# An adaLN attention and sparse-FFN kernel: full shapes for the last group's expert marks, and a new order of work on four engines

## The chip, the cores and the metric

The kernel runs on one core of a Trainium2 chip. The metric is the device time of one execution in microseconds (us): 114.97 us before the change, the median of three executions (114.91 to 114.98).

## The reference, cut to what matters

One transformer block over 2048 tokens of width 128. The values stay in full f32 precision, which the kernel reaches by splitting each operand into a rounded high part and a low rest.

```python
h = layernorm(x) * (1 + ca) + sa
q, k, v = (h @ Wq + bq) / sqrt(128), h @ Wk + bk, h @ Wv + bv
x = x + ga * (softmax(causal(q @ k.T)) @ v @ Wo + bo)
h = layernorm(x) * (1 + cb) + sb
prob = softmax(h @ w_router + b_router)         # 16 expert blocks of 32 channels
mask = top 4 blocks of each token
y = relu(h @ w1.T + b1)                         # 512 channels
x = x + gb * ((y * mask of its block) @ w2.T + b2)
```

## The kernel before, in words

The tokens are worked in four groups of 512 (`GW`), each of four tiles of 128. The order of work is written out by hand: for each engine a plan (`TENSOR_PLAN`, `SCALAR_PLAN`, `VECTOR_PLAN`, `GPSIMD_PLAN`) lists words, a letter for a step and a number for which one. Each engine runs its words strictly in that order, and semaphores hold an instruction until its inputs are there. So a word that waits holds all words behind it on its engine.

The words that matter here, on TensorE: `z` prepares weights, `n` turns a normalized group so that channels are on partitions (4 transposes), `q` projects queries, `a` scores 128 rows to find the row maxima, `b` turns those maxima, `p` and `s` make the score tiles that are used, `w` multiplies the exponentials of a tile by the values, `o` is the output projection, `r` the router's logits, `m` turns the choice of experts, `h` computes 128 hidden channels of a group (4 per group, h12 to h15 for the last), `v` closes the channels of unchosen experts, `d` multiplies by w2, `y` turns the result back, `t` computes the last two tiles in another way. Nearly all matmuls are three passes over 512 columns (L928, L929, L932: high by high, low by high, high by low).

On ScalarE `e` are the exponentials, `a` the normalizations, `c` the copy of the attention sums, `m` the copy of the turned choice, `h` the high part of a hidden chunk, `y` the copy of a result. On GpSimd (POOL) `z` makes constants, `j` and `p` compute the inverse square roots for the norms, `u` splits the tokens, `l` makes the low part of an exponential tile (L512), `k` the low part of a hidden chunk (L518). On VectorE `g` are the norm's statistics, `s` the row maxima, `i` the causal mask on a tile, `x` the output of attention, `m` and `c` the choice of four experts, `h` the masked hidden chunk, `k` and `f` low parts and final sums.

The first three groups multiply the hidden values by a mask (`keep`, [128 channels x 512 tokens]) on VectorE. The last group does it on TensorE: `choose` marks the experts a token did not choose (`unchosen`, 16 columns a tile), `turn_choice` transposes these marks (word m3, L1103, 4 transposes of 16 columns), ScalarE copies them to `shut` (16 partitions x 512), and `shut_channels` (words v12 to v15, L1133) adds a matmul of `spread` (16 x 128, with -1e30 at each expert's channels) by `shut` to the hidden chunk before the relu. This matmul contracts over 16 rows only, in bf16, between matmuls that contract over 128 rows in f32. `spread` is made at the start by GpSimd's word z4 (L502 to L507).

Of the kernel before, what the change touches and what calls it, by code (L numbers as in the profile page):

```python
# [42 lines left out]
TENSOR_PLAN = """
i1 i0 i3 z0 i2 z10 z1 n0 z2 z6 z3 q0 z4 z7 a0 a1 a2 a3 n1 p2 p1 p0 b0 q1 s0 s1 a4 a5 z5 s2 a6 s3 a7 n2 w0 a8 a9
w1 w2 w3 a10 a11 p4 z9 p6 z8 b1 q2 o0 n3 s4 a12 p5 a13 s5 s6 a14 s7 a15 a16 w4 s8 a17 w5 a18 s9 a19 q3 a20 s10
a21 w6 a22 s11 a23 w7 a24 w8 b2 w9 a25 w10 s12 a26 s13 a27 s14 w11 s15 a28 a29 w12 s16 o1 s17 s18 s19 a30 a31
s20 w13 s21 a32 w14 a33 s22 a34 w15 a35 s23 w16 a36 a37 w17 w18 a38 a39 n4 w19 w20 b3 w21 r0 w22 s24 s25 h0 z11
s26 w23 s27 s28 m0 s29 w24 n5 o2 s30 s31 h1 s32 r1 w25 w26 w27 h2 s33 w28 s34 w29 m1 w30 h3 n6 s35 s36 s37 r2
s38 w31 w32 w33 h4 w34 w35 w36 s39 m2 w37 w38 w39 h5 d0 o3 d1 d2 d3 h6 h7 d4 h8 d5 h9 d6 n7 d7 h10 r3 d8 h11 d9
d10 m3 y0 h12 v12 h13 v13 y1 d11 h14 v14 h15 v15 d12 d13 y2 d14 d15 t0 y3 t1  # L50
"""
# [6 lines left out]
VECTOR_PLAN = """
j0 z0 j1 a0 z1 a1 g1 z3 u0 u1 z10 g2 v1 s0 s1 s2 s3 q0 n1 b0 g3 s4 s5 z5 s6 s7 q1 s8 s9 s10 s11 n2 b1 x0 s12 s13
s14 q2 s15 s16 n3 s17 i8 s18 s19 i9 s20 s21 i10 s22 s23 s24 i11 b2 s25 z6 s26 s27 q3 s28 s29 g4 x1 g5 s30 i20  # L60
s31 s32 s33 s34 s35 i21 s36 s37 i22 s38 s39 n4 i23 b3 m0 c0 h0 x2 n5 g6 h1 m1 c1 n6 i36 h2 h3 i37 m2 i38 c2 i39
h4 h5 x3 g7 h6 h7 h8 h9 n7 h10 m3 c3 h11 f0 k12 k13 f1 k14 k15 f2 f3 t0 t1
"""
GPSIMD_PLAN = """
z0 z1 z4 j0 j1 u0 p1 z7 p2 z6 z8 l0 l1 l2 p3 u1 z11 u2 l4 l5 l6 l7 l8 l9 z10 l10 l12 l13 l14 l15 l16 l17 l18 p4
l19 l20 l21 p5 l22 z9 u3 l24 l25 l26 l27 l28 l29 l30 p6 l31 k0 l32 l33 k1 l34 l35 l36 k2 l37 l38 k3 k4 k5 p7 k6
k7 k8 k9 k10 k11 z12
"""
# [1206 lines left out]
```

## Time and profile before

| | before |
|---|---|
| time, median of 3 executions | 114.97 us |
| span of the profiled execution | 113.2 us |
| busy: TensorE | 109.0 us (96%) |
| busy: GpSimd | 88.1 us (78%) |
| busy: VectorE | 87.3 us (77%) |
| busy: ScalarE | 74.3 us (66%) |
| chain that ended last | TensorE 81%, VectorE 13%, issue 2%, GpSimd 2% |

The span runs from the first to the last instruction of the program in the profiled execution. The measured time holds 1.8 us more than it (114.97 less 113.2), which is the launch and end around the program; a time of its own is not given for the profiled execution, so its span stands for it. The busy time of TensorE contains waits that the profile cannot separate, since the ends of matmuls are modelled. What an instruction there really took is read from start to start.

### The profile page before, as it was taken

What the parts mean: (1) busy time and instruction counts of PE and PEld (TensorE: products, weight loads), DVE (VectorE), ACT (ScalarE), POOL (GpSimd) and SP (SyncE); (2) the same over time, 40 slices, a digit from 0 to 9 for tenths busy, and PEclk for the clock granted to TensorE, in tenths of its full rate; (3) what the DMA queues carried; (4) which work ended last, traced back from release to release, by engine and by line L of the source; (5) the groups of instructions that cost most, each with busy time, mean ns of one, the idle gap of its engine ahead of it and who ended that gap; (6) DMA issues with size and microseconds to landing.
All of it is one profiled execution on the core that took longest, in us unless ns stands there. A gap on an engine that the chain in (4) does not pass through costs nothing.

```text
span 113.2 us, 2012 instructions
## 1 busy us (share of the span) xinstructions
PE 109.0 (96%) x585; PEld 87.6 (77%) x585; DVE 87.3 (77%) x322; ACT 74.3 (66%) x163; POOL 88.1 (78%) x118
## 2 busy tenths in 40 slices
PE   5999999999999999999999999999999999999991
PEld 2588769878888888888877878788898888856590
DVE  5999989999999999978897399708974846854251
ACT  1346398497973499677498995988815578435610
POOL 6869868998999199989899999999992898916000
PEclk9999999999999999999999999999999999999999
DMA  2894000000000000000000000000000000003314
GB/s 60 266 336 130 3 0 6 0 3 0 0 3 0 6 0 0 0 0 3 0 0 6 0 0 0 0 0 0 0 6 3 0 3 0 0 0 93 98 56 129
DMA packets 5879, 3.42 MB, mean 30 GB/s; under 512 B 743, under 2 KB 5483, under 8 KB 5868
## 3 DMA queue, kind: packets, MB, share of 16 engines
q1 hardware_dynamic: 5292, 3.03, 9.0%
q10 hardware_dynamic: 576, 0.26, 0.9%
q8 instruction: 5, 0.08, 0.3%
q14 instruction: 6, 0.05, 0.1%
HBM read 2.24 MB, written 1.05 MB: 29 GB/s over the span
## 4 chain that ended last, share of the span: by engine, by line
PE 81%; DVE 13%; issue 2%; POOL 2%
PE bank L928 14%; PE bank L929 13%; PE bank L932 13%; PE bank L1040 7%; PE bank L988 7%; PE bank L1027 6%; PE bank L1028 6%; PE bank L1072 3%; PE bank L962 2%; PE bank L1168 2%; PE bank L1139 2%; DVE nmax L743 1%; DVE st L686 1%; POOL rstd L440 1%; PE bank L1133 1%
## 5 line engine op out<-in xcount | busy, mean ns | idle before, releaser
L512 POOL TENSOR_TENSOR p_lo<-p_full,p_hi 128x512 fp32r<-128x512 f32 (+2 forms) x36 | 42.5, 1206 | 4.6 <-ACT p_full L626 4.5
L619 ACT ACTIVATE p_hi<-bank 128x512 fp32r<-128x512 f32 (+2 forms) x36 | 20.6, 571 | 6.6 <-PE bank L932 2.9
L626 ACT ACTIVATE p_full<-bank 128x512 f32<-128x512 f32 (+2 forms) x36 | 20.5, 568 | 0.6 <-POOL p_lo L512 0.6
L518 POOL TENSOR_TENSOR hid_lo<-hid_full,hid_hi 128x512 fp32r<-128x512 f32 x12 | 15.4, 1294 | 5.3 <-ACT hid_hi L655 5.3
L748 DVE TENSOR_REDUCE cmax<-bank 128x1 f32<-128x512 f32 x24 | 16.1, 685 | 2.0 <-PE bank L988 1.7
L1027 PE MATMUL bank<-g_hi,zt_hi 128*128 128x512 f32 (+3 forms) x40 | 15.2, 381 | 0.0
L1040 PE MATMUL bank<-g_lo,zt_hi 128*128 128x512 f32 (+3 forms) x40 | 14.6, 373 | 0.2 <-DVE g_lo L768 0.2
L1028 PE MATMUL bank<-g_hi,zt_lo 128*128 128x512 f32 (+3 forms) x40 | 14.6, 364 | 0.0
L928 PE MATMUL bank<-p_hi,z_hi 128*128 128x512 f32 (+2 forms) x36 | 14.0, 389 | 0.0
L988 PE MATMUL bank<-zt_hi,g_hi 128*128 128x512 f32 (+3 forms) x40 | 13.8, 386 | 0.0
L929 PE MATMUL bank<-p_hi,z_lo 128*128 128x512 f32 (+2 forms) x36 | 13.5, 374 | 0.0
L932 PE MATMUL bank<-p_lo,z_hi 128*128 128x512 f32 (+2 forms) x36 | 13.4, 373 | 0.0
L841 DVE SCALAR_TENSOR_TENSOR hid_full<-bank,keep 128x512 f32<-128x512 f32 x12 | 8.1, 686 | 5.6 <-POOL hid_lo L518 2.7
L590 ACT ACTIVATE xn<-x,mean_rstd,rstd 128x127 f32<-128x127 f32 x24 | 9.9, 485 | 0.3 <-POOL mean_rstd L433 0.3
L655 ACT CAST hid_hi<-hid_full 128x512 fp32r<-128x512 f32 x12 | 7.4, 622 | 3.0 <-DVE hid_full L841 2.4
L1040 PEld LDWEIGHTS bank<-g_lo,zt_hi 128*128 128x128 f32 x40 | 7.5, 188 | 1.8 <-issue 0.7
L988 PEld LDWEIGHTS bank<-zt_hi,g_hi 128*128 128x128 f32 x40 | 7.5, 189 | 1.4 <-ACT g_hi L605 0.2
L1027 PEld LDWEIGHTS bank<-g_hi,zt_hi 128*128 128x128 f32 x40 | 7.5, 189 | 1.1
L1028 PEld LDWEIGHTS bank<-g_hi,zt_lo 128*128 128x128 f32 x40 | 7.6, 189 | 0.9
L430 POOL TENSOR_TENSOR rstd<-rstd,pow_half 128x4 f32<-128x4 f32 x7 | 7.3, 1038 | 0.6
L928 PEld LDWEIGHTS bank<-p_hi,z_hi 128*128 128x128 f32 x36 | 6.8, 188 | 1.2
L932 PEld LDWEIGHTS bank<-p_lo,z_hi 128*128 128x128 f32 x36 | 6.8, 188 | 1.2
(212 smaller groups left out, 256.1 us busy)
## 6 DMA issues: line engine op xcount, KB each, us to landing
x<-in_L_attn_y_all_dram SPq DMA_DIRECT2D x3, 256.0 KB, 3.5
out_dram<-res SPq DMA_DIRECT2D x3, 256.0 KB, 2.3
w<-in_L_ffn_w_dram SPq DMA_DIRECT2D x2, 256.0 KB, 4.2
x<-in_L_attn_y_all_dram SPq DMA_DIRECT2D x2, 128.0 KB, 2.9
wmod<-in_L_wmod_dram SPq DMA_DIRECT2D x1, 256.0 KB, 3.7
wmod<-in_L_wmod_dram ACTq DMA_DIRECT2D x1, 128.0 KB, 3.2
out_dram<-res SPq DMA_DIRECT2D x1, 128.0 KB, 1.9
wk<-in_L_attn_Wk_dram SPq DMA_DIRECT2D x1, 64.0 KB, 2.9
```

Of the source, the lines that this page charges most:

```text
L512: pool.tensor_tensor(p_lo[:, s, w:], p_full[:, n % 2, w:], p_hi[:, s, w:].bitcast(F32), ALU.subtract).then_inc(p_lo_pool, 1)
L518: pool.tensor_tensor(hid_lo[:, m, :], hid_full[:, n % 2, :], hid_hi[:, m, :].bitcast(F32), ALU.subtract).then_inc(hid_lo_pool, 1)
L619: nc.scalar.activation(p_hi[:, s, w:], src, ACT.Exp).then_inc(p_hi_s, 1)
L626: nc.scalar.activation(p_full[:, n % 2, w:], src, ACT.Exp).then_inc(p_full_s, 1)
L748: nc.vector.tensor_reduce(cmax[:, n, c:c + 1], src, AX.X, ALU.max, negate=True).then_inc(turn_out, 1)
L928: mm(dst, w_hi, m_hi, start=start, stop=False)
L929: mm(dst, w_lo, m_hi, start=False, stop=False)
L932: return mm(dst, w_hi, m_lo, start=False, stop=stop)
L988: last = mm(dst[:, 0:w], tile(g_hi, g * GT + r), zt_hi[:, c * GW:c * GW + w], start=True, stop=not masked)
L1027: mm(dst[:, w:], tile(zt_hi, j), high, start=True, stop=False)
L1028: mm(dst[:, w:], tile(zt_lo, j), high, start=False, stop=False)
L1040: last = mm(dst[:, w:], tile(zt_hi, j), g_lo[:, g * GW + w:(g + 1) * GW], start=False, stop=not diag)
```

## The change

The marks and the pattern of the last group are widened with zeros and with the pattern's own continuation to the whole array: `unchosen` has 128 columns a tile, of which 112 are zeroed once at the start by GpSimd, `spread` and `shut` have 128 partitions. The rows beyond the 16th of `shut` are zero, so the sum is the same. The wait for `spread` moves from v12 to m3. All four plans hold the same words as before, in another order.

```diff
-        shut, spread = sb("shut", [NBLK, GW], BF16), sb("spread", [NBLK, P], BF16)
-        spread_full = sb("spread_full", [NBLK, P])
-        unchosen = sb("unchosen", [P, GT, NBLK], BF16)
+        shut, spread = sb("shut", [P, GW], BF16), sb("spread", [P, P], BF16)
+        spread_full = sb("spread_full", [P, P])
+        unchosen = sb("unchosen", [P, GT, P], BF16)
...
                 elif i == 4:
+                    ahead(pool.memset(unchosen[:, :, NBLK:], 0.0))
                     step(pool.memset(spread_full[:], FAR))
...
-                    nc.scalar.copy(shut[:], norm_bank[0:NBLK, 0:GW // 2].bitcast(BF16)).then_inc(keep_s, 1)
+                    nc.scalar.copy(shut[:], norm_bank[:, 0:GW // 2].bitcast(BF16)).then_inc(keep_s, 1)
...
-                    nc.vector.tensor_scalar(unchosen[:], marked[:, :, 0:NBLK], FURTHEST, None, ALU.is_lt).then_inc(chosen_s, 1)
+                    nc.vector.tensor_scalar(unchosen[:, :, 0:NBLK], marked[:, :, 0:NBLK], FURTHEST, None, ALU.is_lt).then_inc(chosen_s, 1)
...
                 if g in shut_by_tensor:
+                    pe.wait_ge(spread_made, 1)
                     for i in range(GT):
-                        last = nc.tensor.transpose(norm_bank[0:NBLK, i * P // 2:(i + 1) * P // 2].bitcast(BF16),
+                        last = nc.tensor.transpose(norm_bank[:, i * P // 2:(i + 1) * P // 2].bitcast(BF16),
                                                    unchosen[:, i], ident_b[:])
...
                 pe.wait_ge(keep_s, n // NH + 1)
-                if n == NH * shut_by_tensor[0]:
-                    pe.wait_ge(spread_made, 1)
                 mm(turned_bank(f"h{n}")[:], spread[:], shut[:], start=False, stop=True).then_inc(turn_mm, 1)
...
 GPSIMD_PLAN = """
-z0 z1 z4 j0 j1 u0 p1 z7 p2 z6 z8 l0 l1 l2 p3 u1 z11 u2 l4 l5 l6 l7 l8 l9 z10 l10 l12 l13 l14 l15 l16 l17 l18 p4
-l19 l20 l21 p5 l22 z9 u3 l24 l25 l26 l27 l28 l29 l30 p6 l31 k0 l32 l33 k1 l34 l35 l36 k2 l37 l38 k3 k4 k5 p7 k6
+z0 z7 z4 j0 j1 z1 p1 u0 p2 z6 l0 l1 l2 p3 u1 u2 z8 l4 l5 l6 l7 z10 l8 l9 l10 z11 l12 l13 l14 l15 l16 p4 l17
+l18 p5 l19 l20 l21 l22 u3 l24 z9 l25 l26 l27 l28 p6 l29 l30 l31 l32 k0 l33 k1 l34 l35 l36 l37 l38 k2 k3 k4 k5
```

Line numbers shift by one behind the inserted line of word z4 (L502), by two behind the wait inserted in `turn_choice`, and by none again behind the two lines taken out of `shut_channels`, so L928, L929, L932 of before are L929, L930, L933 of the changed kernel, and L1103 is L1105; L1133 and L1168 keep theirs.

TensorE near the end, before: m3 (L1103), y0 (L1168), h12, v12 (L1133), h13, v13, y1.

```order
L1103 MATMUL bank<-ident_b,unchosen 16x128 x4
L1168 MATMUL bank<-ident,y_sb 128x128 x4
L928 MATMUL bank<-h_hi,w1t_hi 128x512
L929 MATMUL bank<-h_hi,w1t_lo 128x512
L932 MATMUL bank<-h_lo,w1t_hi 128x512
L1133 MATMUL bank<-shut,spread 128x512
L928 MATMUL bank<-h_hi,w1t_hi 128x512
L929 MATMUL bank<-h_hi,w1t_lo 128x512
L932 MATMUL bank<-h_lo,w1t_hi 128x512
L1133 MATMUL bank<-shut,spread 128x512
L1168 MATMUL bank<-ident,y_sb 128x128 x4
```

The same place in the changed kernel, from the last pass of d9: y0, m3 (L1105), h13, y1, v12 and v13.

```order
L933 MATMUL bank<-hid_lo,w2t_hi 128x512
L1168 MATMUL bank<-ident,y_sb 128x128 x4
L1105 MATMUL bank<-ident_b,unchosen 128x128 x4
L929 MATMUL bank<-h_hi,w1t_hi 128x512
L930 MATMUL bank<-h_hi,w1t_lo 128x512
L933 MATMUL bank<-h_lo,w1t_hi 128x512
L1168 MATMUL bank<-ident,y_sb 128x128 x4
L1133 MATMUL bank<-shut,spread 128x512 x2
```

h12 now stands ahead of d9, the transposes y0 ahead of m3, d10 behind v13, and v12 and v13 follow each other; v14 and v15 still stand alone.

GpSimd at the start of the program, before: z1 (`causal`), z4 (`spread`), and the first inverse square root (j0).

```order
L470 MEMSET causal_full 128x128
L471 AFFINE_SELECT causal_full<-causal_full 128x128
L473 CAST causal<-causal_full 128x128
L502 MEMSET spread_full 16x128
L503 AFFINE_SELECT spread_full<-spread_full 16x128
L505 AFFINE_SELECT spread_full<-spread_full 16x128
L507 CAST spread<-spread_full 16x128
L439 TENSOR_SCALAR rstd<-mv 128x2
```

In the changed kernel: z7 (`future`), the widened z4, j0.

```order
L475 MEMSET future 128x128
L476 AFFINE_SELECT future<-future 128x128
L502 MEMSET unchosen 128x4x112
L503 MEMSET spread_full 128x128
L504 AFFINE_SELECT spread_full<-spread_full 128x128
L506 AFFINE_SELECT spread_full<-spread_full 128x128
L508 CAST spread<-spread_full 128x128
L439 TENSOR_SCALAR rstd<-mv 128x2
```

Ahead of j0 three instructions of `causal` gave way to two of `future` and a memset of 4x112 elements.

GpSimd in the middle, before: l10 to l18 with p4 behind l18 (`p_lo` is a low part of exponentials, L428 to L433 the inverse square root of a second norm).

```order
L512 TENSOR_TENSOR p_lo<-p_full,p_hi 128x512 x7
L428 TENSOR_SCALAR neg_mean<-mv 128x4
L429 TENSOR_SCALAR rstd<-mv 128x4
L430 TENSOR_TENSOR rstd<-rstd,pow_half 128x4
L433 TENSOR_TENSOR mean_rstd<-neg_mean,rstd 128x4
L512 TENSOR_TENSOR p_lo<-p_full,p_hi 128x512 x2
L512 TENSOR_TENSOR p_lo<-p_full,p_hi 128x384
```

In the changed kernel: l12 to l16, p4, l17, l18, p5.

```order
L513 TENSOR_TENSOR p_lo<-p_full,p_hi 128x512 x5
L428 TENSOR_SCALAR neg_mean<-mv 128x4
L429 TENSOR_SCALAR rstd<-mv 128x4
L430 TENSOR_TENSOR rstd<-rstd,pow_half 128x4
L433 TENSOR_TENSOR mean_rstd<-neg_mean,rstd 128x4
L513 TENSOR_TENSOR p_lo<-p_full,p_hi 128x512 x2
L428 TENSOR_SCALAR neg_mean<-mv 128x4
```

Both inverse square roots now stand ahead of l19, which had only p4 ahead of it.

## Rows read from the trace of the kernel before

**Rows 1.** The page, busy time of each engine (us, share of span, instructions).

```profile
PE 109.0 (96%) x585; PEld 87.6 (77%) x585; DVE 87.3 (77%) x322; ACT 74.3 (66%) x163; POOL 88.1 (78%) x118
```

**Rows 2.** The waits of TensorE: who waited for whom, total us, times, longest.

```profile
PE bank L1182 <- DVE lift L876: 0.2, 1, 0.2
PE bank L1040 <- DVE g_lo L768: 0.2, 1, 0.2
```

**Rows 3.** TensorE's timeline at v12 and v15: start us, us, instruction.

```profile
101.29 0.39 PE L932 MATMUL bank<-h_lo,w1t_hi 128*128 128x512 f32 x1
101.61 0.38 PE L1133 MATMUL bank<-shut,spread 16*128 16x512 bf16 x1
101.92 0.50 PE L928 MATMUL bank<-h_hi,w1t_hi 128*128 128x512 f32 x1
102.25 0.39 PE L929 MATMUL bank<-h_hi,w1t_lo 128*128 128x512 f32 x1
...
106.00 0.40 PE L932 MATMUL bank<-h_lo,w1t_hi 128*128 128x512 f32 x1
106.33 0.39 PE L1133 MATMUL bank<-shut,spread 16*128 16x512 bf16 x1
106.64 0.39 PE L928 MATMUL bank<-hid_hi,w2t_hi 128*128 128x256 f32 x1
106.88 0.28 PE L929 MATMUL bank<-hid_hi,w2t_lo 128*128 128x256 f32 x1
```

**Rows 4.** TensorE's timeline at m1, full-shape bf16 transposes of an earlier group.

```profile
73.47 0.39 PE L932 MATMUL bank<-p_lo,z_hi 128*128 128x512 f32 x1
73.70 0.40 PE L1108 MATMUL bank<-ident_b,chosen 128*128 128x128 bf16 x4
73.91 0.48 PE L928 MATMUL bank<-p_hi,z_hi 128*128 128x512 f32 x1
74.23 0.39 PE L929 MATMUL bank<-p_hi,z_lo 128*128 128x512 f32 x1
```

**Rows 5.** Timeline of the weight loads at m1 and at v12.

```profile
73.70 0.23 PEld L1108 LDWEIGHTS bank<-ident_b,chosen 128*128 128x128 bf16 x4 [0.26 <-issue]
...
101.60 0.09 PEld L1133 LDWEIGHTS bank<-shut,spread 16*128 16x128 bf16 x1 [0.36 <-issue]
```

**Rows 6.** TensorE's timeline ahead of m3 and behind y0, and around y2.

```profile
99.68 0.40 PE L932 MATMUL bank<-hid_lo,w2t_hi 128*128 128x512 f32 x1
...
101.06 0.39 PE L929 MATMUL bank<-h_hi,w1t_lo 128*128 128x512 f32 x1
...
107.47 0.60 PE L1168 MATMUL bank<-ident,y_sb 128*128 128x128 f32 x4
...
108.03 0.28 PE L929 MATMUL bank<-hid_hi,w2t_lo 128*128 128x256 f32 x1
```

**Rows 7.** GpSimd's timeline at the start.

```profile
0.36 0.10 POOL L1262 MEMSET const-bfloat16-1.0<- 128x1 bf16 x1
...
1.51 0.21 POOL L470 MEMSET causal_full<- 128x128 f32 x1
...
2.46 0.20 POOL L502 MEMSET spread_full<- 16x128 f32 x1
2.73 0.99 POOL L503 TENSOR_SCALAR_AFFINE_SELECT spread_full<-spread_full 16x128 f32<-16x128 f32 x1
...
4.14 0.28 POOL L507 CAST spread<-spread_full 16x128 bf16<-16x128 f32 x1
4.67 0.25 POOL L439 TENSOR_SCALAR rstd<-mv 128x2 f32<-128x2 f32 x1 [0.25 <-DVE mv L698]
```

**Rows 8.** Timelines in the middle: GpSimd's p4 and l19 to l21, TensorE's last pass of w20.

```profile
48.76 0.24 POOL L428 TENSOR_SCALAR neg_mean<-mv 128x4 f32<-128x4 f32 x1
...
50.65 3.58 POOL L512 TENSOR_TENSOR p_lo<-p_full,p_hi 128x512 fp32r<-128x512 f32 x3
...
55.64 0.40 PE L932 MATMUL bank<-p_lo,z_hi 128*128 128x512 f32 x1
```

More of the change, by code:

```diff
@@ L43 @@
 TENSOR_PLAN = """
[L44 to L48, printed above, removed]
@@ L49 @@
-s38 w31 w32 w33 h4 w34 w35 w36 s39 m2 w37 w38 w39 h5 d0 o3 d1 d2 d3 h6 h7 d4 h8 d5 h9 d6 n7 d7 h10 r3 d8 h11 d9
-d10 m3 y0 h12 v12 h13 v13 y1 d11 h14 v14 h15 v15 d12 d13 y2 d14 d15 t0 y3 t1
+i1 i0 i3 z0 i2 z10 z1 n0 z2 z3 q0 z4 z6 a0 a1 a2 p0 a3 n1 z7 b0 p1 q1 p2 s0 s1 a4 a5 z5 s2 a6 s3 a7 w0 a8 n2
+a9 w1 w2 w3 a10 a11 p4 z9 p6 z8 b1 q2 o0 n3 s4 a12 p5 a13 s5 s6 a14 s7 a15 a16 s8 w4 a17 s9 a18 w5 a19 q3 a20
+s10 a21 w6 a22 s11 a23 w7 a24 w8 b2 w9 w10 s12 a25 s13 w11 a26 s14 a27 s15 o1 s16 s17 a28 w12 a29 s18 a30 s19
@@ L51 @@
+s20 a31 a32 w13 w14 a33 s21 a34 w15 a35 n4 a36 w16 a37 s22 w17 a38 s23 a39 w18 w19 w20 b3 r0 w21 s24 w22 w23
+s25 s26 s27 o2 s28 m0 s29 w24 h0 h1 n5 w25 z11 w26 s30 s31 s32 r1 h2 w27 s33 w28 s34 s35 w29 m1 s36 h3 w30 n6
+s37 w31 s38 w32 h4 s39 r2 w33 w34 w35 w36 w37 w38 w39 h5 d0 m2 o3 d1 d2 d3 h6 h7 d4 d5 h8 h9 d6 n7 h10 d7 r3
+d8 h11 h12 d9 y0 m3 h13 y1 v12 v13 d10 d11 h14 v14 h15 v15 d12 d13 d14 y2 d15 t0 y3 t1
 """
 SCALAR_PLAN = """
-z0 z1 j0 j1 z3 z6 z11 q0 z4 n1 z9 a2 q1 e0 z5 e1 e2 n2 e3 c0 z13 z12 a3 z8 q2 e4 n3 e5 e6 e7 e8 q3 e9 e10 e11
@@ L54 @@
-e12 e13 c1 e14 e15 e16 z7 e17 e18 e19 e20 a4 e21 n4 e22 e23 a5 e24 e25 e26 c2 m0 e27 e28 e29 n5 e30 h0 e31 e32
-a6 h1 e33 m1 e34 n6 e35 e36 e37 z14 h2 h3 e38 e39 c3 h4 m2 h5 y0 h6 h7 a7 h8 n7 h9 y1 h10 m3 h11 h12 h13 y2 h14
-h15 y3 z15
+z0 z1 j0 j1 z3 q0 z11 z4 z6 n1 a2 q1 e0 z9 z5 e1 e2 e3 z13 c0 n2 z12 a3 q2 z8 e4 e5 e6 n3 e7 e8 e9 q3 e10 e11
+e12 c1 e13 e14 e15 e16 e17 e18 a4 e19 z7 e20 n4 e21 e22 e23 e24 c2 e25 e26 a5 e27 m0 e28 n5 h0 e29 e30 e31 h1
+e32 e33 e34 a6 m1 h2 e35 n6 e36 e37 e38 z14 h3 e39 c3 m2 h4 h5 y0 h6 h7 a7 h8 n7 y1 h9 h10 h11 m3 h12 h13 y2
@@ L57 @@
+h14 h15 y3 z15
 """
 VECTOR_PLAN = """
[L59 to L62, printed above, removed]
+j0 z0 j1 a0 z1 a1 g1 u0 z3 u1 z10 g2 v1 s0 s1 s2 s3 q0 n1 b0 g3 s4 s5 z5 s6 s7 q1 s8 s9 s10 s11 n2 b1 x0 s12
@@ L63 @@
+s13 s14 q2 s15 s16 n3 s17 i8 s18 s19 i9 s20 s21 i10 s22 s23 s24 b2 i11 s25 s26 s27 g4 x1 s28 z6 s29 s30 g5 s31
+s32 s33 s34 i20 s35 i21 s36 s37 n4 s38 s39 i22 q3 b3 i23 m0 c0 x2 h0 g6 h1 n5 m1 c1 i36 h2 i37 i38 n6 h3 m2
+i39 c2 h4 h5 x3 g7 h6 h7 h8 h9 n7 h10 m3 c3 h11 f0 f1 k12 k13 k14 k15 f2 t0 f3 t1
 """
 GPSIMD_PLAN = """
-z0 z1 z4 j0 j1 u0 p1 z7 p2 z6 z8 l0 l1 l2 p3 u1 z11 u2 l4 l5 l6 l7 l8 l9 z10 l10 l12 l13 l14 l15 l16 l17 l18 p4
-l19 l20 l21 p5 l22 z9 u3 l24 l25 l26 l27 l28 l29 l30 p6 l31 k0 l32 l33 k1 l34 l35 l36 k2 l37 l38 k3 k4 k5 p7 k6
@@ L67 @@
-k7 k8 k9 k10 k11 z12
+z0 z7 z4 j0 j1 z1 p1 u0 p2 z6 l0 l1 l2 p3 u1 u2 z8 l4 l5 l6 l7 z10 l8 l9 l10 z11 l12 l13 l14 l15 l16 p4 l17
+l18 p5 l19 l20 l21 l22 u3 l24 z9 l25 l26 l27 l28 p6 l29 l30 l31 l32 k0 l33 k1 l34 l35 l36 l37 l38 k2 k3 k4 k5
+p7 k6 k7 k8 k9 k10 k11 z12
 """
```

## Prediction

> **What bounds the kernel now.** I read the page's busy times first. TensorE is busy for 109.0 of 113.2 us, and no other engine passes 78% [rows 1]. Such a busy time can hide waits, so the waits of TensorE come next: there are only two behind the opening, of 0.2 us each, for the first `lift` (L1182) and for the first shift in `g_lo` (L1040), both in the first 16 us [rows 2]. So behind the head TensorE issues one matmul after the other, and the end moves with the sum of its steps. A moved word gains nothing there by itself; it can only lose, where it comes before its input. The third view is TensorE's timeline, read from start to start: three passes of 512 columns follow each other at 0.23 us (73.47 to 73.70, [rows 4]). What takes longer than its columns is lost time that the busy figure hides, and the few bf16 matmuls over 16 rows are such places [rows 3]. VectorE and GpSimd matter in two ways: in the head, where TensorE waits for them, and in the middle, where GpSimd makes the low parts that TensorE reads.
>
> **The full shapes, on TensorE.** The change neither adds nor removes a matmul. In the place of v12 (L1133 by 16 rows) the passes around it start at 101.29, 101.61, 101.92 and 102.25 [rows 3]. From the L932 to the L929 behind it that is 0.96 us. The two f32 passes in it are worth 2 x 0.23 = 0.46, so the visit costs 0.50. Around v15 it is 106.00 to 106.88, 0.88 us; less 0.23 and less 0.12 (256 columns are half of 512) it is 0.53. There are four such visits; at the mean of the first and the last, 0.515, they take 2.06 us.
>
> What they take in full shape is shown by no L1133, but by a bf16 group of the same 512 columns between the same f32 passes: m1, four transposes of 128 columns with all rows and columns. From 73.47 to 74.23 it is 0.76 us; less 0.46 the visit costs 0.30 [rows 4]. The weight loads say why the two differ. At m1 the load starts at 73.70, just as the pass ahead has had its 0.23; at v12 it starts at 101.60, 0.08 behind the 0.23 of the pass ahead (101.29 + 0.23 = 101.52) [rows 3, 5]. Behind v12 the next pass starts 0.31 after it instead of 0.23, and the one after that again 0.33 later. So a partial shape is paid for on entry and on leaving, 0.08 each, and its successor's weights are loaded late as well; a full shape in bf16 pays for its own load alone.
>
> In the changed order v12 and v13 follow each other, so the pair enters once: 0.30 + 0.23 = 0.53. v14 and v15 stand alone, 0.30 each. The sum is 1.13, and the four visits save 2.06 - 1.13 = 0.93 us.
>
> m3 has its 16 columns on the other side, in its output. From the L932 at 99.68 to the L929 at 101.06 it is 1.38 us [rows 6]. In it are two passes, 0.46, and the four transposes of y0, which I price at y2's: 107.47 to 108.03 is 0.56, less the 0.12 of one pass of 256 columns, 0.44. So m3 costs 1.38 - 0.46 - 0.44 = 0.48. As m1 it costs 0.30, a saving of 0.18.
>
> Together 1.11 us. These are all in the last 14 us, where each step stands on the path to the end. Bounds: if the bf16 load hides as well, a v costs its 0.23 alone, four cost 0.92, and m3 costs 0.23: a saving of 1.39. If shape has no part in it, only the pairing helps, 0.515 - 0.23 = 0.29. I take 1.1, since m1 has the types, the columns and the neighbours of the case.
>
> The late load at 101.60 [rows 5] stands against a rule of the Trainium skill, "TensorE: Matmul & The Clock Gate", Step-by-step: what each phase is for: the time of a weight load goes by its number of columns, and its number of rows does not matter. By that rule the widening of `spread` from 16 to 128 rows gains nothing, and the time would be that of the first rival below; by the rows it is that of the sum.
>
> **What the others do for it.** ScalarE's copy `shut` and VectorE's `unchosen` keep their free sizes (512 and 64 elements a partition), so I cost them at nothing. The wait for `spread` ahead of m3 is for something made a hundred microseconds before. v12 waits for ScalarE's copy, which now stands behind the cast h11; in between TensorE has h13 (0.69) and y1 (0.44), and I expect this cover to hold.
>
> **GpSimd's start.** Ahead of the first inverse square root (L439, 4.67) GpSimd idles 0.25 us, from the end of `spread` at 4.42 [rows 7]. Three instructions of `causal` took 1.51 to 2.46, 0.95 us; two of `future` I take at two thirds of that, 0.63. Then comes a memset of 448 elements. One of 1 element takes 0.10, one of 128 elements 0.20, so 448 take 0.10 + 448/128 x 0.10 = 0.45. That makes 1.08 for 0.95, 0.13 later, within the 0.25: nothing. Lower bound 0.20 (a memset does not get slower by length), also nothing. Upper bound: it takes as long as the slowest elementwise instruction of GpSimd in any row here, one split of 512 (3.58 for 2.75 of them, 1.30) [rows 8]: then L439 is 0.63 + 1.30 - 0.95 - 0.25 = 0.73 late, and since the first normalization, the turn and the scores hang on it, so is the end. The affine select of 0.99 us (2.73) is a riddle, as its twin behind it takes 0.3; if it is a collision it can swallow the delay or double it. I take 0.
>
> **The orders.** In the head w1's preparation (z6, z7) moves behind the first query projection and the first maxima. The wait for `g_lo` (0.2) is set by VectorE, whose words there stay but for one swap, so I take 0; at best both waits of [rows 2] go, -0.4. In the middle the tightest place that I find is GpSimd's. Before, p4 alone stands ahead of l19; now p4 and p5 do. p4 takes 48.76 to 50.65, 1.89 us. l19 to l21 then run 50.65 to 54.23, l20 ends at about 50.65 + 2 x 1.30 = 53.25 [rows 8]. With another 1.89 ahead it ends at 55.14. TensorE's w20 reads it in its last pass at 55.64 [rows 8], and the words ahead of w20 on TensorE are the same as before. So 0.5 us of cover is left: cost 0, bound +0.5 if the estimate of GpSimd's queue is 1 us short. ScalarE's a4 now stands ahead of e19 and needs p4; it makes e19 later, and l19 can't start before e19, but l19 is already behind p5.
>
> **The sum.** 113.2 - 1.1 = 112.1 us of span. The measured median stands 1.8 above the span before (1.77), and nothing around the program changes: 113.9 us.
>
> **The rivals.**
> - *Type, not shape.* The lost time at v12 comes from going between f32 and bf16, in whatever shape. Then only the pairing of v12 and v13 gains, 0.29: 114.7 us. Against it stands m1, the same change of type at 0.30 instead of 0.50. For it: no full bf16 matmul of 512 columns stands between f32 passes in this trace. 5%.
> - *The memset is on the head's path.* GpSimd reaches L439 up to 0.73 late: 113.9 + 0.3 to 0.7, 114.2 to 114.6. For it: only 0.25 of idle time, and a select of 0.99 that nothing explains. 13%.
> - *The new orders wait in several places.* The full saving comes, but TensorE, which had no waits behind the head, gets some of 0.1 to 0.2 each where words come earlier than before: half of the gain is lost, 114.2 to 114.7. 9%.
> - *GpSimd's queue becomes the bound in the middle (the slower side).* Both p4 and p5 ahead of l19, and l19 held by e19, which ScalarE reaches only when a4 has had p4's result. The cover at w20 is 0.5. Up to there it costs nothing, beyond it each microsecond costs one; the change turns slower when GpSimd is 0.5 + 1.1 = 1.6 us later than I count. Were p5 to start only after a further p-length (1.89), it would be 1.4 lost against 1.1 gained: 115.3 us. Against it: p5's input comes from VectorE early, by the place that its word has there. 5%.
>
> **How the numbers follow.** The forecast has 68%, with its own range of 113.5 to 114.2: the saving of 1.39 instead of 1.1 and the waits of the head make the low end, some 0.3 of small waits the high one. With the rivals at 5, 13, 9 and 5% the range for 8 in 10 is 113.4 to 114.5, which leaves out the top of the second and third rival and most of the first and the fourth. About 0.2% (0.23 us) is what a measurement of this kernel tells from no change. Faster than that: the forecast 68, the second rival 13, the third 8, half of the first 2: 90 or so, which I round down to 0.88, for what I have not seen in four rewritten orders. The same 0.06, slower 0.06.
>
> **What would show it.** Right: the L1133 are of form 128x512, the step from the pass ahead into them is 0.23, from the load of L1133 to the next f32 load there is almost no time, and from the passes around one v it is 0.76 instead of 0.96; the stretch from d9 to the first of t0 shrinks by about 1.1; TensorE's list of waits has nothing new above 0.2; L439 starts at 4.7. Wrong: L1133 still 0.31 long with a late load behind it (first rival); the start of L439 and all of VectorE's head shifted alike (second); new waits of TensorE for GpSimd's `p_lo` between 50 and 60 us (fourth), or for ScalarE's `shut` ahead of v12.

## The result and the profile after

The change makes the kernel slower: 115.75 us (median of four executions, 115.72 to 115.82) against 114.97 (now four executions, 114.91 to 115.23), a ratio of 1.0065 with a 95% interval of 1.0048 to 1.0081. Forecast was 113.9, so 1.85 us are missing. The profiled execution has a span of 114.0 us and took 115.72.

The busy times, against [rows 1], say little. TensorE is busy for 0.5 us less, where run 1, with the shapes alone, is 1.2 us less busy. VectorE has 2.0 us more, with the same 322 instructions of the same sizes, and that is the first hint:

```profile
PE 108.5 (95%) x585; PEld 87.3 (77%) x585; DVE 89.3 (78%) x322; ACT 74.5 (65%) x163; POOL 89.1 (78%) x119
```

**Where the time went.** Three places of TensorE's program have the same work ahead of them in both orders (but for one or two words): the third pass of s0, m0's transposes and t0. Timeline of TensorE, kernel before and then kernel after:

```profile
15.53 0.47 PE L1040 MATMUL bank<-g_lo,zt_hi 128*128 128x512 f32 x1 [0.19 <-DVE g_lo L768]
...
61.95 0.40 PE L1108 MATMUL bank<-ident_b,chosen 128*128 128x128 bf16 x4
...
108.61 0.39 PE L1139 MATMUL bank<-w_full,hid_last 128*128 128x128 f32 x2
```

```profile
16.45 0.47 PE L1041 MATMUL bank<-g_lo,zt_hi 128*128 128x512 f32 x1
...
63.66 0.40 PE L1110 MATMUL bank<-ident_b,chosen 128*128 128x128 bf16 x4
...
109.45 0.49 PE L1139 MATMUL bank<-w_full,hid_last 128*128 128x128 f32 x3
```

The delay is 0.92 at s0, 1.71 at m0 and 0.84 at t0. At r3, where the last stretch begins, it is still 1.74 (96.22 and 97.96). So the head loses 0.9, the middle another 0.8 (0.2 of the head comes back behind s0, so the middle's own loss is 1.0), and the end gains 0.9, where the shapes alone gain 1.3 (run 1) and a new stall costs 0.3 (runs 9 and 10).

**The end.** TensorE's timeline at v12 and v13, then at v14:

```profile
103.48 0.60 PE L1168 MATMUL bank<-ident,y_sb 128*128 128x128 f32 x4
103.92 0.59 PE L1133 MATMUL bank<-shut,spread 128*128 128x512 bf16 x2
...
104.58 0.39 PE L930 MATMUL bank<-hid_hi,w2t_lo 128*128 128x512 f32 x1
...
106.20 0.40 PE L933 MATMUL bank<-h_lo,w1t_hi 128*128 128x512 f32 x1
106.44 0.39 PE L1133 MATMUL bank<-shut,spread 128*128 128x512 bf16 x1
...
106.91 0.39 PE L930 MATMUL bank<-h_hi,w1t_lo 128*128 128x512 f32 x1
```

From L933 at 106.20 to L930 at 106.91 it is 0.71 with one L1133 in it, where [rows 3] have 0.96. Less two passes of 0.23, a visit costs 0.25 instead of the 0.50 there. What is read is the step over the visit and the pass behind it, since L929's modelled start (106.48) moves with the shape.

**The waits name little of the loss.** TensorE's list of waits, against [rows 2]:

```profile
PE bank L1182 <- DVE lift L877: 0.5, 1, 0.5
PE bank L963 <- DVE xn L714: 0.3, 1, 0.3
...
PE bank L929 <- DVE hid_full L842: 0.2, 1, 0.2
```

What explains it are durations. Three instructions of VectorE (one of v1's, the sum z6, the marks) and one of GpSimd took 1.4 to 5.4 times as long as the same instruction in the kernel before, each beside an instruction of the other of these two engines. Durations of v1 (four instructions), of the marks and of the sum of two rows (ns, lowest, median, highest), kernel before and then kernel after; the last line is GpSimd's low parts:

```profile
L713 DVE TENSOR_SCALAR xn<-x,mv,rstd x4: 316/338/352, 10.9 to 11.7; 128x127 f32<-128x127 f32 x4
L826 DVE TENSOR_SCALAR unchosen<-marked x1: 194/194/194, 99.3 to 99.3; 128x64 bf16<-128x64 f32 x1
L889 DVE TENSOR_TENSOR w_full<-w_full,b_row x1: 1059/1059/1059, 38.7 to 38.7; 1x512 f32<-1x512 f32 x1
L512 POOL TENSOR_TENSOR p_lo<-p_full,p_hi x36: 729/1294/1332, 17.3 to 83.4; 128x512 fp32r<-128x512 f32 x28, 128x384 fp32r<-128x384 f32 x4, 128x256 fp32r<-128x256 f32 x4
```

```profile
L714 DVE TENSOR_SCALAR xn<-x,mv,rstd x4: 333/342/993, 11.2 to 12.6; 128x127 f32<-128x127 f32 x4
L827 DVE TENSOR_SCALAR unchosen<-marked x1: 1044/1044/1044, 101.0 to 101.0; 128x64 bf16<-128x64 f32 x1
L890 DVE TENSOR_TENSOR w_full<-w_full,b_row x1: 1515/1515/1515, 45.4 to 45.4; 1x512 f32<-1x512 f32 x1
L513 POOL TENSOR_TENSOR p_lo<-p_full,p_hi x36: 736/1295/2149, 18.2 to 83.9; 128x512 fp32r<-128x512 f32 x28, 128x384 fp32r<-128x384 f32 x4, 128x256 fp32r<-128x256 f32 x4
```

What GpSimd did meanwhile, from its timeline of the kernel after, beside v1 and beside the marks (what it did beside z6 stands with run 7):

```profile
10.78 1.28 POOL L445 TENSOR_TENSOR z_lo<-xn,z_hi 128x512 fp32r<-128x512 f32 x1
...
99.43 2.54 POOL L519 TENSOR_TENSOR hid_lo<-hid_full,hid_hi 128x512 fp32r<-128x512 f32 x2 [1.22 <-ACT hid_hi L656]
```

The marks start at 100.98 and take 1.04, to 102.02; GpSimd's pair ends at 99.43 + 2.54 = 101.97. So they seem not to have run slowly but to have stood still until GpSimd was done. In the kernel before, the same split u0 ran from 8.19, 1.27 long, and had ended before v1 began at 10.90.

My theory after these traces: the new orders put one-source and two-source VectorE instructions that work in SBUF beside GpSimd's splits, and one stands still for the other. The rivals: the orders place words of TensorE ahead of their inputs; or the wider shapes cost something elsewhere.

### The profile page after: what moved, and what is told of

Its sections match the earlier page's. It is cut to its first block, busy times and chain, and to the rows that moved or that the text cites. A ratio compares the mean times of both kernels' runs of the same rounds, so it can differ in the third digit from the quotient of the medians.

```text
span 114.0 us, 2013 instructions
## 1 busy us (share of the span) xinstructions
PE 108.5 (95%) x585; PEld 87.3 (77%) x585; DVE 89.3 (78%) x322; ACT 74.5 (65%) x163; POOL 89.1 (78%) x119
## 4 chain that ended last, share of the span: by engine, by line
PE 67%; DVE 12%; POOL 6%; DMA 4%; issue 4%; SPq 3%; ACT 1%; DVEq 0%
PE bank L929 10%; PE bank L933 10%; PE bank L930 10%; PE bank L1041 7%; PE bank L989 6%; PE bank L1028 6%; PE bank L1029 6%; POOL hid_lo L519 4%; DMA x<-in_L_attn_y_all_dram 4%; SPq L370 3%; PE bank L1073 2%; PE bank L963 2%; DVE hid_full L842 2%; PE bank L1139 2%; DVE xn L714 1%
## 5 line engine op out<-in xcount | busy, mean ns | idle before, releaser
L513 POOL TENSOR_TENSOR p_lo<-p_full,p_hi 128x512 fp32r<-128x512 f32 (+2 forms) x36 | 43.2, 1227 | 5.1 <-ACT p_full L627 4.8
L989 PE MATMUL bank<-zt_hi,g_hi 128*128 128x512 f32 (+3 forms) x40 | 14.8, 387 | 0.1
L929 PE MATMUL bank<-p_hi,z_hi 128*128 128x512 f32 (+2 forms) x36 | 13.8, 382 | 0.0
L933 PE MATMUL bank<-p_lo,z_hi 128*128 128x512 f32 (+2 forms) x36 | 13.6, 377 | 0.0
L930 PE MATMUL bank<-p_hi,z_lo 128*128 128x512 f32 (+2 forms) x36 | 13.5, 374 | 0.0
L933 PEld LDWEIGHTS bank<-p_lo,z_hi 128*128 128x128 f32 x36 | 6.8, 188 | 1.5 <-POOL p_lo L513 0.3
L930 PEld LDWEIGHTS bank<-p_hi,z_lo 128*128 128x128 f32 x36 | 6.8, 188 | 1.0
```

What stands on the lines that cost most here:

```text
L513: pool.tensor_tensor(p_lo[:, s, w:], p_full[:, n % 2, w:], p_hi[:, s, w:].bitcast(F32), ALU.subtract).then_inc(p_lo_pool, 1)
L929: mm(dst, w_hi, m_hi, start=start, stop=False)
L930: mm(dst, w_lo, m_hi, start=False, stop=False)
L933: return mm(dst, w_hi, m_lo, start=False, stop=stop)
L989: last = mm(dst[:, 0:w], tile(g_hi, g * GT + r), zt_hi[:, c * GW:c * GW + w], start=True, stop=not masked)
```

## The experiments

Twelve kernels ran. "Difference" is against the runs of the kernel before in the same comparison.

| run | edit | median us (runs) | before | difference | ratio, 95% interval |
|---|---|---|---|---|---|
| 1 | full shapes, all old orders | 113.68 (5) | 114.98 | -1.30 | 0.9846 to 0.9894 |
| 2 | new orders, narrow shapes | 116.61 (6) | 114.98 | +1.63 | 1.0105 to 1.0149 |
| 3 | after, GpSimd's head as before | 114.85 (12) | 114.98 | -0.13 | 0.9964 to 0.9991 |
| 4 | before, u0 behind p1 | 115.62 (11) | 114.98 | +0.64 | 1.0032 to 1.0060 |
| 5 | run 1 with the new late orders | 113.99 (9) | 114.90 | -0.91 | 0.9896 to 0.9948 |
| 6 | run 5, h9 ahead of y1 | 113.75 (6) | 114.90 | -1.15 | 0.9867 to 0.9923 |
| 7 | run 3, z6 of VectorE as before | 114.28 (6) | 114.90 | -0.62 | 0.9922 to 0.9966 |
| 8 | run 7, a25 and n4 as before | 115.72 (6) | 114.90 | +0.82 | 1.0043 to 1.0096 |
| 9 | run 7, a25 as before | 113.94 (5) | 114.86 | -0.92 | 0.9906 to 0.9933 |
| 10 | run 9, h9 ahead of y1 | 113.65 (4) | 114.86 | -1.21 | 0.9879 to 0.9906 |
| 11 | best of the parts | 113.33 (4) | 114.86 | -1.53 | 0.9857 to 0.9884 |
| 12 | run 1, fewer rows in three visits | 114.44 (1) | 114.86 | -0.42 | none |

**Runs 1 and 2: shapes and orders apart.** Run 1 is the diff without its plans, run 2 the plans without the rest.

> The four full shapes, with all four orders as before. Theory (the new orders cost time, the shapes gain what the changed kernel's end shows): with v12 to v15 apart as before, each visit costs 0.24 instead of 0.515, so the four save 1.1 and m3 0.2: 114.97 - 1.3 = 113.7 us, 113.5 to 114.0. Rival (full shapes also slow something elsewhere, the memset in the head or the wait ahead of m3): above 114.4. Rival (only the pairing of v12 and v13 gained): 114.7 or more, with a v still costing 0.5.

> The four new orders alone, with the narrow shapes as before. Theory: the changed kernel's 115.75 plus what the shapes give there, 0.9 to 1.2 us (v12 and v13 paired leave one entry less): 116.7 to 117.0 us. Rival (the orders are harmless, the shapes cost): 115.0 or less. Rival (orders and shapes each cost a part): between 115.2 and 116.2.

113.68 is in the range of its theory, 116.61 is 0.09 below the range of its own; both refute their rivals. The shapes alone gain 1.30 and the memset and the early wait for `spread` cost nothing that is seen (why, is said under GpSimd's start below); the orders alone cost 1.63. Together they give +0.78 and not 1.63 - 1.30 = +0.33, so in the new orders the shapes gain only 0.85. Run 2's timeline shows why: h13's first pass starts at the same 102.68 as in the kernel after, and VectorE's h11, which it waits for by the list of the kernel after, ends at 102.62 or 102.63 in both, so what m3 saves is lost there; and with v12 and v13 side by side the pair saves one entry, not two.

```profile
102.68 0.50 PE L928 MATMUL bank<-h_hi,w1t_hi 128*128 128x512 f32 x1
...
103.48 0.60 PE L1168 MATMUL bank<-ident,y_sb 128*128 128x128 f32 x4
104.01 0.60 PE L1133 MATMUL bank<-shut,spread 16*128 16x512 bf16 x2
...
104.88 0.40 PE L929 MATMUL bank<-hid_hi,w2t_lo 128*128 128x512 f32 x1
```

From 103.48 to L929 at 104.88 it is 1.40, in the kernel after from 103.48 to L930 at 104.58 it is 1.10: 0.30 for the pair, and 0.28 each for v14 and v15 make 0.86.

**Runs 3 and 4: the head.** Run 3 gives the changed kernel GpSimd's old first ten words; run 4 moves one word in the kernel before.

```diff
 GpSimd, run 3
-z0 z7 z4 j0 j1 z1 p1 u0 p2 z6 l0
+z0 z1 z4 j0 j1 u0 p1 z7 p2 z6 l0
 GpSimd, run 4
-z0 z1 z4 j0 j1 u0 p1 z7 p2
+z0 z1 z4 j0 j1 p1 u0 z7 p2
```

> The changed kernel with GpSimd's first ten words in the order of before, so that u0 (the split of the first tokens) runs ahead of p1 and has ended when VectorE's v1 starts. Theory (v1 ran slow, 1.77 instead of 1.10 us, because GpSimd's split ran beside it, both reading SBUF): v1 is back at 1.10 and the scores s0 start 0.6 to 0.7 earlier; part of it may be lost behind it: 115.1 to 115.3 us. Rival (v1 is slow for another reason, such as its rows or the late x): v1 stays at 1.7 and the time at 115.7. Rival (the head recovers by itself, since the middle is bound elsewhere): v1 at 1.10, but the time at 115.6 or more.

> The kernel before, with one word moved: GpSimd's u0 behind p1 instead of ahead of it, so that u0 stands beside VectorE's v1. Theory (contention of the two engines on SBUF): the four instructions of v1 take 1.6 to 1.8 us instead of 1.10, the scores start 0.5 later, and the time is 115.2 to 115.5 us. Rival (no contention): v1 stays at 1.10; p1 ends earlier by u0's 2 us but the normalization waits for other things, so the time is 114.8 to 115.0 us.

Run 3 came to 114.85, 0.91 better than the kernel after and more than I had expected: it takes back all of the head's 0.92. Run 4 came to 115.62, 0.64 worse, a little beyond the range of its theory, by one word. These are run 4's v1 and GpSimd's timeline beside it:

```profile
L713 DVE TENSOR_SCALAR xn<-x,mv,rstd x4: 334/379/1312, 10.9 to 12.6; 128x127 f32<-128x127 f32 x4
```

```profile
10.72 1.27 POOL L445 TENSOR_TENSOR z_lo<-xn,z_hi 128x512 fp32r<-128x512 f32 x1
```

One of the four took 1.31 us. It is the first, from 10.90 to 12.21, while L445 ran until 10.72 + 1.27 = 11.99. VectorE's four now take 2.03 instead of 1.10, and nothing else was touched. This settles the head. The x that arrived 0.30 late in the profile of the kernel after was no part of it: in run 4 it is not late, and s0 is 0.92 late all the same.

**Runs 5 and 6: the marks.** Run 5 has full shapes and the old orders up to about 84 us, the new ones behind; run 6 exchanges one pair in it.

```diff
 ScalarE, run 6
-h6 h7 a7 h8 n7 y1 h9 h10 h11 m3
+h6 h7 a7 h8 n7 h9 y1 h10 h11 m3
```

> The full shapes; the orders of before up to some 84 us, and the changed kernel's orders behind that on all four engines (from h4/s39 on). Against the first run (full shapes, all orders of before, 113.68). Theory (ScalarE's y1 ahead of h9 makes GpSimd's k9 and k10 some 1.3 us late, and VectorE's marks, a one-source operation on f32 in SBUF, stand still until k10 has ended): the marks take 1.04 instead of 0.19 us, and the time is 0.3 to 0.4 above the first run: 114.0 to 114.1 us. Rival (the late order gains the entry that the pairing of v12 and v13 saves, and the marks' 1.04 comes from the delay of the middle): marks at 0.19, 113.4 to 113.6 us.

> As the run before it, with one pair of words exchanged on ScalarE: h9 ahead of y1, as in the kernel before. Theory (collision of the marks with GpSimd's k10): k10 has ended when the marks start, they take 0.19 us, and the stall of 0.3 ahead of h13 goes: 113.5 to 113.8 us. Rival (the stall at h13 comes from the order on TensorE, with h12 and h13 placed earlier, whatever the marks do): marks at 0.19, but the time stays at 114.0.

Both theories hold: 113.99 stands 0.01 below its range, 113.75 is inside. The executions of run 6 scatter from 113.45 to 114.44, so its 0.24 alone would be weak; the durations are not, and the same pair gives 0.29 between runs 9 and 10, which scatter less. The marks and GpSimd's k10, run 5 and then run 6:

```profile
99.16 1.05 DVE L827 TENSOR_SCALAR unchosen<-marked 128x64 bf16<-128x64 f32 x1
```

```profile
97.61 2.55 POOL L519 TENSOR_TENSOR hid_lo<-hid_full,hid_hi 128x512 fp32r<-128x512 f32 x2 [1.27 <-ACT hid_hi L656]
```

```profile
99.48 0.20 DVE L827 TENSOR_SCALAR unchosen<-marked 128x64 bf16<-128x64 f32 x1
```

```profile
98.19 1.29 POOL L519 TENSOR_TENSOR hid_lo<-hid_full,hid_hi 128x512 fp32r<-128x512 f32 x1 [0.29 <-ACT hid_hi L656]
```

In run 5 the marks end at 100.21 and GpSimd at 100.16. In run 6 GpSimd ends at 99.48, as the marks start. ScalarE's y1 ahead of h9 made GpSimd wait 1.27 for its input; that wait cost nothing on GpSimd itself, but it moved k10 onto the marks.

**Runs 7, 8 and 9: the middle.**

```diff
 VectorE, run 7
-i11 s25 s26 s27 g4 x1 s28 z6 s29 s30
+i11 s25 z6 s26 s27 g4 x1 s28 s29 s30
 TensorE, runs 8 and 9
-b2 w9 w10 s12 a25 s13
+b2 w9 a25 w10 s12 s13
 TensorE, run 8 alone
-w15 a35 n4 a36 w16 a37 s22 w17 a38 s23 a39 w18
+w15 a35 a36 w16 a37 s22 w17 a38 s23 a39 n4 w18
```

> The third run's kernel (the changed kernel with GpSimd's head as before, 114.85 us), with VectorE's z6 (the sum of two 1x512 rows) back in its place behind s25. Theory: z6 is off the way of s30, a32 no longer waits for s30, and some 0.2 to 0.3 of the middle's 1.05 comes back: 114.5 to 114.7 us. Rival (a32's wait is covered by the later one at n4, which stays): 114.8 to 114.9 us.

> The run before it with two words of TensorE also put back: a25 between w9 and w10 (so that s12 comes 0.24 later and b2's shift is there), and n4 behind a39 instead of behind a35 (so that ScalarE's a4 has ended). Theory (the middle loses its 1.05 us by three waits of TensorE that its new order meets too early): most of it comes back, 0.7 to 1.0 against the third run: 113.9 to 114.2 us. Rival (GpSimd's queue bounds the middle, both inverse roots p4 and p5 standing ahead of l19, whatever TensorE does): under 0.3 comes back, 114.6 or more.

> The run before last (the changed kernel with GpSimd's head and VectorE's z6 as before, 114.28 us), with one word of TensorE put back: a25 between w9 and w10; n4 stays where the change has it. Theory (s12 meets b2's shift 0.24 us too early, and the loss of the last run came from n4 alone, which holds ScalarE's queue and through it GpSimd's when it comes late): 0.2 to 0.3 comes back, 114.0 to 114.1 us. Rival (a25 itself was part of the loss of the run before): 114.5 or more.

Run 7 gave back 0.49 (-0.62 against run 3's -0.13), twice what I had expected. The larger part of it is VectorE's own lateness. These are TensorE's a31 and a32, run 3 and then run 7:

```profile
46.87 0.91 PE L989 MATMUL bank<-zt_hi,g_hi 128*128 128x256 f32 x2
```

```profile
46.94 0.51 PE L989 MATMUL bank<-zt_hi,g_hi 128*128 128x256 f32 x2
```

The next pass starts at 47.62 and at 47.28, so the two take 0.75 in the one and 0.34 in the other: 0.41 is lost ahead of a32, which waits for VectorE's s30. That ends at 47.23 in run 3 and at 46.47 in run 7. z6 took 1.53 in run 3 and takes 1.06 in run 7. By an estimate from these numbers s30 would have ended at 46.76 without the 0.47 of stall, in time for a32, so this loss too is the stall's and not that of z6's place.

z6 did harm on the other engine as well. GpSimd's l14 to l16 and p4 behind them, kernel after and then run 7:

```profile
43.41 4.65 POOL L513 TENSOR_TENSOR p_lo<-p_full,p_hi 128x512 fp32r<-128x512 f32 x3
48.14 0.24 POOL L428 TENSOR_SCALAR neg_mean<-mv 128x4 f32<-128x4 f32 x1
```

```profile
42.75 3.81 POOL L513 TENSOR_TENSOR p_lo<-p_full,p_hi 128x512 fp32r<-128x512 f32 x3
46.64 0.23 POOL L428 TENSOR_SCALAR neg_mean<-mv 128x4 f32<-128x4 f32 x1
```

The three take 4.65 instead of 3.81, that is 0.84 more, and it is all in the last (2.149 us, the highest above, against 1.30). z6's start was at 45.37; it stood still until l15 was done at 45.97, ended at 46.89, and in between l16 stood still for it. So p4 came late, and behind p4 ScalarE's a4 and TensorE's n4 (from the pass ahead of n4 to the one behind it is 0.70 in run 3 and 0.53 in run 7). In run 7 z6 still meets one split, at 39.65 (1.907 us is that run's highest). What it costs there was not separated.

Run 8 is my miss: expected 113.9 to 114.2, measured 115.72, 1.44 worse than run 7. I had read the step at n4 as "TensorE comes too early" and moved n4 back by eight words. But ScalarE's n4 stands where the change put it, ahead of e21, and now held that engine:

```profile
54.21 0.59 ACT L602 CAST h_hi<-bank 128x512 fp32r<-128x512 f32 x1 [1.72 <-PE bank L963]
```

In run 7 this cast starts at 52.60 without a wait. The wait alone does not tell its price, since the same cast waits 1.56 in the kernel before. TensorE loses most of the time at b3, 1.27 behind the start of the pass ahead at 55.85:

```profile
57.12 0.30 PE L1005 MATMUL bank<-ident,nmax 128*128 128x128 f32 x1 [0.88 <-DVE nmax L759]
```

The links from ScalarE's cast to these row maxima of VectorE were not followed. Run 9 leaves n4 alone and puts only a25 back: 113.94, 0.30 better than run 7 against its own runs of before, as forecast. With a25 ahead of it the third pass of s12 finds VectorE's low part ready. TensorE's timeline at s12, kernel after and then run 9:

```profile
38.48 0.39 PE L1029 MATMUL bank<-g_hi,zt_lo 128*128 128x512 f32 x1
38.88 0.47 PE L1041 MATMUL bank<-g_lo,zt_hi 128*128 128x512 f32 x1
```

```profile
37.81 0.40 PE L1029 MATMUL bank<-g_hi,zt_lo 128*128 128x512 f32 x1
38.05 0.42 PE L1041 MATMUL bank<-g_lo,zt_hi 128*128 128x512 f32 x1
```

The step from the second to the third pass is 0.40 in the one and 0.24 in the other. In run 7 it is 0.40 too, and s13 starts 0.22 later there than in run 9 (38.52 and 38.30). The rest of the 0.30 is not assigned: in run 9 z6 has also moved off the split that it met in run 7, which takes 1.29 again. By runs 8 and 9 a late n4 costs 0.82 + 0.92 = 1.74 us; the new place of n4 is better than the late one, given the other three plans.

**Runs 10 and 11: the parts together.** Run 10 is run 9 with run 6's pair exchanged. Run 11 has full shapes, the new head orders of TensorE, ScalarE and VectorE (to s1, e2 and v1) with GpSimd's old one, the old middle, and run 6's late orders.

> The run before it, and ScalarE's h9 ahead of y1. These four moves are what I hold the orders' loss to be: u0 beside v1, z6 beside GpSimd's low parts, s12 ahead of b2's shift, and the marks beside k10. Theory: the marks take 0.19, the stall ahead of h13 goes, 113.7 to 113.9 us, that is, the new orders with four words put back are no worse than the old ones (113.68 with full shapes). Rival (more waits lie behind these): 114.0 or more.

> A version meant to beat both: full shapes; the new orders of the head on TensorE, ScalarE and VectorE (up to s1, e2, s0), where the third run was 0.2 ahead of the kernel before, GpSimd's head as before; the middle of before; the new late orders with ScalarE's h9 ahead of y1. Theory: 113.68, less 0.2 for the head, less 0 to 0.2 for the pairing of v12 and v13: 113.3 to 113.5 us. Rival (what the head gains is waited for again in the middle, whose orders fit the old head): 113.6 to 113.8 us.

Run 10 at 113.65, 0.05 under the range of its theory, says that four places hold the orders' whole loss: it is where the old orders are with full shapes (113.68). Run 11 at 113.33 beats both kernels, by 1.53 against the one before and some 2.3 against the one after. TensorE's list of waits in run 11 has only its first, during the start:

```profile
PE bank L1244 <- DVE filler L905: 1.2, 1, 1.2
```

**Run 12: how many rows.**

```diff
-mm(turned_bank(f"h{n}")[:], spread[:], shut[:], start=False, stop=True)
+rows = (128, 64, 32, 16)[n % NH]
+mm(turned_bank(f"h{n}")[:], spread[0:rows], shut[0:rows], start=False, stop=True)
```

> Full shapes with all orders of before, but the last group's four closing matmuls take 128, 64, 32 and 16 rows (v12, v13, v14, v15); the rows left out hold zeros, so nothing of the result changes. One look at the steps on TensorE from the pass ahead to the pass behind. Theory (what costs is that the array is not used in all its rows, whatever their number): v12 0.23 beyond its neighbours' time, v13, v14 and v15 all 0.5. Rival (the cost grows by steps with fewer rows): 0.23, then between 0.3 and 0.5. Rival (only the columns of the type and not the rows matter, and the widened output of m3 made the gain): all four 0.23.

TensorE's timeline, first run 1 at v14 with 128 rows, then run 12 at v14 and v15 with 32 and 16:

```profile
104.13 0.40 PE L933 MATMUL bank<-h_lo,w1t_hi 128*128 128x512 f32 x1
104.37 0.39 PE L1133 MATMUL bank<-shut,spread 128*128 128x512 bf16 x1
...
104.83 0.40 PE L930 MATMUL bank<-h_hi,w1t_lo 128*128 128x512 f32 x1
```

```profile
104.30 0.40 PE L933 MATMUL bank<-h_lo,w1t_hi 128*128 128x512 f32 x1
104.63 0.39 PE L1134 MATMUL bank<-shut,spread 32*128 32x512 bf16 x1
...
105.28 0.39 PE L930 MATMUL bank<-h_hi,w1t_lo 128*128 128x512 f32 x1
105.51 0.40 PE L933 MATMUL bank<-h_lo,w1t_hi 128*128 128x512 f32 x1
105.84 0.39 PE L1134 MATMUL bank<-shut,spread 16*128 16x512 bf16 x1
106.15 0.39 PE L929 MATMUL bank<-hid_hi,w2t_hi 128*128 128x256 f32 x1
```

Over the visit it is 0.70 with 128 rows and 0.98 with 32: 0.28 more. With 64 rows the steps into the L1134 and out of it are 0.33 and 0.32 (101.99, 102.32, 102.64), with 32 rows 0.33 and 0.32, with 16 rows 0.33 and 0.31. So the price does not go by the number of rows; using fewer than all has one price. It fits the time: three visits at 0.28 are 0.84, and run 12 is 0.88 worse than run 1, each against its own runs of before.

## Why the prediction was wrong

**The shapes: the mechanism was right, the size a little small.** Forecast 1.11 with bounds of 0.29 and 1.39, measured 1.30 in run 1. Run 1 has the four visits apart, where the forecast had two of them paired; by the forecast's own terms it would be 2.06 - 4 x 0.30 + 0.18 = 1.04. The term that was mis-sized is the visit: 0.30 by m1's transposes, measured 0.24. The part that I had put into the bound, "the bf16 load hides as well", is what happens. m3's 0.18 measured 0.23 in run 1. The rival "type, not shape" is refuted: a full bf16 matmul between f32 passes costs its 0.23 alone.

The rule of the Trainium skill that I weighed against the change ("TensorE: Matmul & The Clock Gate", Step-by-step: what each phase is for) agrees with the traces: the weight load of L1133 is 0.10 long with 128 rows and 0.09 with 16. I had read the late start of the load as standing against it, but the rule is of its length. The change gained by the steps into and out of the visit. "TensorEngine Tiling (Array Packing)", Key Properties, of the Trainium skill says that a change of tiling mode drains TensorE, and its modes include 64 and 32 rows; run 12's equal price for 64, 32 and 16 rows fits that, but no run shows the drain itself.

**GpSimd's start: right.** The memset took 0.47 (0.45 estimated), and the first inverse root L439 starts at 4.67 as in [rows 7]. The second rival (13%) did not happen. But the cover is more than the 0.25 of idle time that I counted. Run 1 keeps `causal` ahead and adds the memset, and there the select of 0.99 in [rows 7] takes the delay up:

```profile
3.13 0.59 POOL L504 TENSOR_SCALAR_AFFINE_SELECT spread_full<-spread_full 128x128 f32<-128x128 f32 x1
```

It starts 0.40 later than in the kernel before and ends as it did, at 3.72 or 3.73, like every trace here, whether it starts at 2.37 (run 2) or at 3.14 (run 9). So it is held by something. VectorE's memset of 1024 columns (2.59 to 3.50) and ScalarE's table load (2.30 to 3.58) run beside it in each; which of them holds it was not tested. "If it is a collision it can swallow the delay" came true as far as the swallowing goes.

**The orders: this is the step that failed.** "The orders. In the head ... so I take 0", and "cost 0" in the middle, where the orders cost 1.63. I had looked at an order as a matter of waits, who needs whose result, and priced the one place where a queue looked tight, GpSimd's at l19. That rival (5%) did not come about in this form: w20 was held by nothing. Most of what happened is not in the dependencies. From run to run, each against its own runs of before:

| place | from, to | cost us |
|---|---|---|
| u0 beside v1 | after, run 3 | 0.91 |
| z6 beside l15 and l16 | run 3, run 7 | 0.49 |
| s12 ahead of b2's shift | run 7, run 9 | 0.30 |
| marks beside k10, by y1 ahead of h9 | run 9, run 10 | 0.29 |
| all other moves | run 10, run 1 | 0.09 |

0.78 - 1.99 = -1.21 is run 10, and with the last row -1.30 is run 1. So 1.69 of the 2.08 lie at three places where VectorE and GpSimd stand still for each other, and 0.30 at a wait of the kind that my third rival spoke of. (For z6 this rests on the estimate at run 7.) That rival had the right kind, but at most 0.8 us, and 9%. The last row is a sum of losses and gains: in run 3 TensorE is some 0.2 ahead of the kernel before right behind s0.

The rule was there to be read. "SBUF — State Buffer", in the section SBUF: two separate sides, of the Trainium skill says that one port pair is shared by VectorE and GpSimd as an exclusive lock, "not a bandwidth split": a VectorE instruction takes it when it runs in a mode with two ports, or when it has two SBUF inputs and the GpSimd instruction reads SBUF, and the loser stands still for the whole instruction. No trace here shows the mode of an instruction. On the standing still the traces agree: 1.31 for 0.34 in run 4, 1.04 for 0.19 at the marks, and 2.15 for 1.30 on GpSimd's side. In the trace of before v1, z6 and the marks all run at full speed. One row did point to an instruction that is held: the select of 0.99 in [rows 7], which I called a riddle and set at 0 without asking what else in the new orders might be held so. The list of the other engine's instructions beside v1, z6 and the marks would have shown it.

**VectorE's and ScalarE's part: the shape right, one place not priced.** "I cost them at nothing" was right for the shape: the marks take 0.195 in run 1 and 0.194 before. "I expect this cover to hold" was said of v12 and ScalarE's copy, and it held: v12 starts 0.44 behind y1, y1's own time. What the forecast did not look at is one place earlier: h13 starts 0.2 late by the list of waits, behind VectorE's h11, which stood behind the marks.

**The chances.** Faster had 88%, and slower 6%. The low doubt about four rewritten orders rested on nothing that I had read in the trace.

## What to carry to other kernels

Before moving an instruction, ask not only who waits for it but what runs beside it: in these runs two forms of VectorE's TENSOR_SCALAR (f32, SBUF to SBUF) and its sum of two rows in SBUF stood still for GpSimd's two-source splits of 512 columns, and the sum held such a split in turn. Such a stall is itself in no list of waits, which show at most what it makes late; compare the highest duration of each form with its median. And a word that is moved on one engine needs its partners moved on the others: n4 moved back alone cost 1.7 us.

## What the runs showed of the hardware

- A VectorE instruction held by GpSimd is recorded as running. Its duration holds the stall, and the median of its group hides it (342 against 993 ns).
- It is held, not slowed: the first of v1 starts at 11.15 in the kernel after and at 10.76 in run 2, beside the same split (10.78 to 12.06 and 12.05), and ends at 12.14 in both. In run 2 it lost although its record starts 0.02 before the split's.
- In the traces of before, after and runs 1, 3 and 4, only three kinds of VectorE instructions, two forms of TENSOR_SCALAR (f32, SBUF to SBUF) and the two-source sum of two rows, ever took over 1.3 times what they take elsewhere. The 125 reductions of 512 columns all took 0.66 to 0.69, beside GpSimd or not. Reading f32 from SBUF is not enough to be held: the 160 norm statistics (BATCH_NORM_STATS2 of 128 columns), 69 of them beside such a split, all took 0.26 to 0.30.
- It goes both ways: GpSimd's split took 2.15 instead of 1.30 behind a one-row sum of 512 elements, which uses a single partition.
- A bf16 matmul of 512 columns in all 128 rows between f32 passes costs 0.24, its own 512 columns; in 32 or 16 rows 0.52, and 64 rows show the same steps of 0.33 and 0.32 (run 12, one execution).
